# The second MLP product of three transformer layers from high and low fp32r parts, both made on VectorE

## What is computed

```python
h = gelu(xm @ W_mlp1 + b_mlp1)      # xm: normed and modulated x, [256, 256]; h: [256, 1024]
y = h @ W_mlp2 + b_mlp2             # the second product: the one that changes
x = x + gate * y
```

## Time and profile before

| | |
|---|---|
| median of 3 runs | 2873.33 us (2870.46 to 2873.42) |
| the profiled execution | 2874.42 us, of which the span from first to last instruction is 2872.6 us |
| PE busy | 2745.2 us, 96% of the span |
| PEld busy | 2279.8 us, 79% |
| DVE busy | 1732.0 us, 60% |
| ACT busy | 1548.3 us, 54% |
| POOL busy | 687.1 us, 24% |
| mean granted clock of TensorE | 0.974 of full speed |

### The profile page before, as it was taken

How to read it: one execution, slowest core, us unless ns; L and a number is a source line. 1 busy time by engine, 2 the same in 40 slices (tenths; PEclk the granted TensorE clock), 3 DMA queues, 4 the chain that set the end, 5 groups by cost and what they waited for, 6 DMA issues and landing times.

```text
span 2872.6 us, 61852 instructions
## 1 busy us (share of the span) xinstructions
PE 2745.2 (96%) x23508; PEld 2279.8 (79%) x23508; DVE 1732.0 (60%) x3584; ACT 1548.3 (54%) x2703; POOL 687.1 (24%) x759
## 2 busy tenths in 40 slices
PE   7999999995899999999999999999999999999998
PEld 6999999993577777777777777777777777777876
DVE  2444444434676776766766667667566666666642
ACT  3444444432456565665566656655566556556553
POOL 3433434321112212222222122222111111111111
PEclk8999999996899999999999999999999999999998
DMA  5122222104434444344464443554546535444421
GB/s 162 45 79 80 70 70 70 40 9 132 95 82 116 100 103 122 94 107 124 106 145 97 98 118 93 112 117 93 128 102 136 115 85 112 103 94 105 103 69 38
DMA packets 276950, 277.90 MB, mean 97 GB/s; under 512 B 90352, under 2 KB 206432, under 8 KB 276656
## 3 DMA queue, kind: packets, MB, share of 16 engines
q1 hardware_dynamic: 264752, 251.26, 36.8%
q10 hardware_dynamic: 11904, 22.68, 2.6%
HBM read 99.03 MB, written 29.56 MB: 45 GB/s over the span
## 4 chain that ended last, share of the span: by engine, by line
PE 64%; DVE 7%; issue 3%; ACT 2%; DMA 1%; SPq 0%; POOL 0%; POOLq 0%; DVEq 0%; ACTq 0%
PE gbank L3183 12%; PE obank L3028 10%; PE gbank L3028 7%; PE obank L3035 6%; PE score L3093 4%; PE obank L3113 4%; DVE m_a L2477 4%; PE obank L3159 3%; PE score L3079 3%; PE score L3142 2%; DVE x_a L2439 2%; PE gbank L3128 2%; PE obank L3128 2%; PE gbank L3019 2%; PE gbank L3043 2%
## 5 line engine op out<-in xcount | busy, mean ns | idle before, releaser
L1971 ACT ACTIVATE p_f<-score 128x1024 f32<-128x1024 f32 (+1 forms) x576 | 567.8, 1021 | 293.7 <-PE score L3093 264.6
L2477 DVE TENSOR_REDUCE m_a<-score 128x4 f32<-128x1024 f32 x384 | 459.9, 1219 | 159.0 <-PE score L3079 158.8
L3183 PE MATMUL gbank<-w,h_c 128*128 128x256 f32 x1536 | 387.9, 392 | 1.9 <-ACT h_c L1988 1.9
L3183 PEld LDWEIGHTS gbank<-w,h_c 128*128 128x128 f32 x1536 | 279.2, 191 | 44.9 <-ACT h_c L1988 2.3
L1150 PE MATMUL m_ps<-m_comb,m_w 128*128 128x256 f32 x2304 | 295.4, 284 | 1.5 <-PEq L254 1.5
L1150 PEld LDWEIGHTS m_ps<-m_comb,m_w 128*128 128x128 f32 x2304 | 279.9, 188 | 5.0 <-issue 3.6
L2487 DVE TENSOR_REDUCE m_b<-gbank 128x4 f32<-128x308 f32 x192 | 92.1, 480 | 265.1 <-PE gbank L3128 241.6
L823 ACT ACTIVATE m_hf<-m_ps,tab 128x256 f32<-128x256 f32 x192 | 80.7, 471 | 246.8 <-PE m_ps L1150 246.8
L1848 POOL TENSOR_TENSOR o_gated<-w_o,gate_a 128x512 f32<-128x512 f32 x48 | 62.3, 1298 | 591.0 <-PE obank L3035 591.0
L765 POOL TENSOR_TENSOR m_hhl<-m_hf,m_hhl 128x512 fp32r<-128x512 f32 x96 | 125.3, 1306 | 318.6 <-DVE m_hhl L989 318.6
L3113 PE MATMUL obank<-p_f,v_s 128*20 128x256 f32 x3072 | 199.9, 390 | 0.6 <-ACT p_f L1971 0.4
(11 more groups left out here) (287 smaller groups left out, 5446.0 us busy)
## 6 DMA issues: line engine op xcount, KB each, us to landing
q_cat<-q_hl SPq DMA_DIRECT2D x288, 128.0 KB, 3.7
k_cat<-k_hl SPq DMA_DIRECT2D x288, 128.0 KB, 4.0
qc_cat<-qc_hl SPq DMA_DIRECT2D x288, 128.0 KB, 3.1
split_L<-m_cut SPq DMA_DIRECT2D x24, 512.0 KB, 5.7
x_a<-x_after_L SPq DMA_DIRECT2D x48, 256.0 KB, 2.7
x_b<-x_after_L SPq DMA_DIRECT2D x48, 256.0 KB, 4.4
kc_cat<-kc_hl SPq DMA_DIRECT2D x288, 39.0 KB, 1.9
x_after_L<-y_c SPq DMA_DIRECT2D x32, 256.0 KB, 2.4
```

What stands on the lines that cost most here:

```text
L1971: e.activation(p_f[i % 4][0:n, :], score[i % 2].ap[0:n, :, :].rearrange("p h n -> p (h n)"), ACT.Exp, scale=SCALE).then_inc(ex.sem, 1)
L2477: e.tensor_reduce(m_a[:, :, i::NPAIR].rearrange("p t h -> p h t"), score[i % 2].ap[:, :, :].rearrange("p h (t k) -> p h t k", t=TT), AX.X, ...
L3183: mm = e.matmul(B_DOWN.ap[:, tt, :], h_c[:, k, tt * P:(tt + 1) * P], weights_of(d)["w2"][:, k, :], start=(k == 0), stop=(k == MC - 1))
```

## The change

ACT writes the gelu's result to a new small buffer `h_f` with two quarters; DVE casts each quarter to fp32r (`mlp_h_high`) and subtracts that from the exact value (`mlp_h_low`), both into a `h_c` with a high and a low plane. `down` makes three fp32r matmuls in place of each fp32 one, and waits per quarter. `up_act` waits until the low part two quarters earlier is made. The `w2` weights become four more pieces a layer: 36 pieces in place of 24, three per iteration of the mixture, still with two buffers; `w_down` is one buffer for all layers, loaded by ACT's queue at the start of `blocks` and at each change of layer.

```diff
+        def pieces_of(n):
+            return range(3 * n - 6, 3 * n - 3)
...
-                for i in range(2):
-                    store_piece(2 * n - 6 + i)
-                    load_piece(2 * n - 4 + i)
+                for k in pieces_of(n):
+                    store_piece(k - 2)
+                    load_piece(k)
...
-        h_c, y_c = sb("h_c", [P, MC, NT]), tile("y_c")
+        h_f, h_c, y_c = sb("h_f", [P, 2, 2, NT]), sb("h_c", [P, 2, MC, NT], F32R), tile("y_c")
...
             def up_act(u, i):
                 gelu = ACT.Gelu if layer(u) == 3 else ACT.Gelu_apprx_tanh
                 e.wait_ge(*S["C_hp"].at(u, i + 1))
-                if u and i == 0:
-                    e.wait_ge(*S["C_down"].at(u - 1))
+                if i >= 2:
+                    e.wait_ge(*S["C_hl"].at(u, i - 1))
+                elif u:
+                    e.wait_ge(*S["C_hl"].at(u - 1, i + 3))
...
+            def next_down(d):
+                if last_of_layer(d):
+                    e.wait_ge(*S["C_down"].at(d))
+                    load_split(layer(d) + 1, "down", "down", 8, (0, 1, 2, 3))
...
+            def mlp_h_high(c, i):
+                if not live(c):
+                    return
+                e.wait_ge(*S["C_h"].at(c, i + 1))
+                if c and i == 0:
+                    e.wait_ge(*S["C_down"].at(c - 1))
+                e.tensor_copy(h_c[:, 0, 2 * i:2 * i + 2, :], h_f[:, i % 2, :, :]).then_inc(S["C_hh"].sem, 1)
+
+            def mlp_h_low(c, i):
+                if live(c):
+                    e.wait_ge(*S["C_hh"].at(c, i + 1))
+                    e.tensor_tensor(h_c[:, 1, 2 * i:2 * i + 2, :], h_f[:, i % 2, :, :],
+                                    h_c[:, 0, 2 * i:2 * i + 2, :].bitcast(F32), ALU.subtract).then_inc(S["C_hl"].sem, 1)
...
             def down(d, j):
                 if not live(d):
                     return
+                tt, i = divmod(j, MC // 2)
                 if j == 0:
-                    e.wait_ge(*S["C_h"].at(d))
+                    weights_in(d, "down")
                     turn(B_DOWN, S["C_y"], d)
-                for i in (2 * j, 2 * j + 1):
-                    tt, k = divmod(i, MC)
-                    mm = e.matmul(B_DOWN.ap[:, tt, :], h_c[:, k, tt * P:(tt + 1) * P], weights_of(d)["w2"][:, k, :],
-                                  start=(k == 0), stop=(k == MC - 1))
+                if tt == 0:
+                    e.wait_ge(*S["C_hh"].at(d, i + 1))
+                for wp, xp in TERMS:
+                    if xp and tt == 0:
+                        e.wait_ge(*S["C_hl"].at(d, i + 1))
+                    for c in range(CC):
+                        mm = e.matmul(B_DOWN.ap[:, tt, :], h_c[:, xp, 2 * i + c, tt * P:(tt + 1) * P],
+                                      W["down"][:, i, wp, c, :], start=(i + wp + xp + c == 0),
+                                      stop=(i == MC // 2 - 1 and xp == 1 and c == CC - 1))
```

More of the change, by code:

```diff
@@ L806, in _ @@
                 hidden_low(g, 5)
-                for i in range(2):
-                    piece_low(2 * n - 4 + i)
+                for k in pieces_of(n):
+                    piece_low(k)
             gated_sum(NB - 1)
@@ L938, in _ @@
                 gate(g)
-                for i in range(2):
-                    piece_high(2 * n - 4 + i)
+                for k in pieces_of(n):
+                    piece_high(k)
         @block.vector
@@ L1904, in _ @@
             self_out_gated(4)
-            for n in range(6, 47):
-                q, a, c, d = n - 1, n - 3, n - 5, n - 6
+            context_rstd(4)
+            mlp_rstd(2)
+            for n in range(7, 47):
+                self_rstd(n - 1)
+                mlp_sum(n - 6)
+                self_residual(n - 3)
+                self_out_gated(n - 2)
+                mlp_residual(n - 5)
+                cross_rstd(n - 3)
+                cross_residual(n - 3)
                 if live(n) and n % NB == 0:
@@ L2145, in first_of_the_rest @@
                 load_split(1, "up1", "up", 4, (2, 3))
+                load_split(1, "down", "down", 8, (0, 1, 2, 3))
             e.wait_ge(s_w[1], 16 * n_w[1])
@@ L2267, in _ @@
             exp_table(1)
-            for n in range(6, 47):
-                q, m, a, b, c = n - 1, n - 2, n - 3, n - 4, n - 5
+            self_weights(4, 5)
+            self_heads(4, 0)
+            next_rest(6)
+            self_weights(4, 6)
+            self_weights(4, 7)
+            cross_max_high(3)
+            self_heads(4, 1)
+            mlp_modulated(2)
+            cross_weights(3, 0)
+            cross_weights(3, 1)
+            cross_weights(3, 2)
+            cross_heads(3, 0)
+            cross_weights(3, 3)
+            gelu_table(2)
+            context_out(4)
+            cross_heads(3, 1)
+            mlp_act(2, 0)
+            mlp_act(2, 1)
+            cross_keys_high(4)
+            mlp_act(2, 2)
+            for n in range(7, 47):
+                self_modulated(n - 1)
+                self_max_high(n - 2)
+                cross_x_out(n - 3)
+                mlp_act(n - 5, 3)
+                keys_high(n - 1)
+                cross_queries_high(n - 3)
+                exp_table(n - 5)
+                queries_high(n - 1)
+                self_weights(n - 2, 0)
+                self_weights(n - 2, 1)
+                self_weights(n - 2, 2)
+                self_weights(n - 2, 3)
+                self_weights(n - 2, 4)
                 if live(n) and n % NB == 0:
@@ L2825, in _ @@
             self_sum(3)
-            for n in range(6, 47):
-                p, q, m, a, b, c, d = n, n - 1, n - 2, n - 3, n - 4, n - 5, n - 6
+            cross_stats(3)
+            self_max(4, 7)
+            mlp_h_high(1, 2)
+            mlp_h_low(1, 2)
+            cross_normed(3)
+            self_x_high(5)
+            self_x_low(5)
+            self_max_low(4)
+            cross_x_low(3)
+            context_stats(4)
+            mlp_h_high(1, 3)
+            mlp_h_low(1, 3)
+            cross_heads_normed(2)
@@ new lines, in _ @@
+            keys_low(5)
+            cross_queries_low(3)
+            cross_sum(2)
+            queries_low(5)
+            mlp_stats(2)
+            cross_max(3, 0, 0)
+            cross_max(3, 0, 1)
+            context_normed(4)
+            cross_max(3, 1, 0)
+            cross_max(3, 1, 1)
+            mlp_normed(2)
+            cross_max(3, 2, 0)
+            cross_max(3, 2, 1)
+            cross_max(3, 3, 0)
+            cross_max(3, 3, 1)
+            for n in range(7, 47):
+                self_stats(n - 1)
+                cross_max_low(n - 4)
+                mlp_gated(n - 6)
+                self_normed(n - 1)
+                self_max(n - 2, 0)
+                self_max(n - 2, 1)
+                mlp_x_high(n - 5)
+                mlp_x_low(n - 5)
+                values_out(n - 2)
+                self_recips(n - 3)
+                self_max(n - 2, 2)
+                self_max(n - 2, 3)
+                self_max(n - 2, 4)
+                mlp_h_high(n - 5, 0)
+                mlp_h_low(n - 5, 0)
+                self_max(n - 2, 5)
+                mlp_h_high(n - 5, 1)
+                mlp_h_low(n - 5, 1)
+                self_heads_normed(n - 3)
+                self_max(n - 2, 6)
+                cross_recips(n - 4)
+                cross_keys_low(n - 3)
+                self_sum(n - 3)
+                cross_values_out(n - 3)
```

332 lines of the change are left out of this document (210 added, 122 removed).

## The result

The changed kernel takes **2910.76 us** (median; 2910.55 to 2913.43). The kernel before took 2871.89 us beside it (2866.67 to 2873.42). The ratio is **1.0135, 95% interval 1.0119 to 1.0152**: slower by 1.4%, about 39 us. Forecast were 2917 us, 2868 to 2952. The total is right, and the largest step of the blocks, the wait for `oT_a`, is right to 0.2 us. But that the sum came out is luck: a term of the mixture that was far too large stood against two costs that were not in it.

A forecast was written before the change was run, and what follows sets the result against it. PE was taken as the bound, with DVE only a few tenths of a microsecond ahead. Profiled 2874.42 us + 15.6 (blocks) + 23 (mixture) + 6 (`w_down` loads) - 1 (end) = 2918 us, 2917 for the median; range 2868 to 2952 us.

The forecast's parts named there:

- the wait for `oT_a`: In `blocks`, two pairs on DVE make PE wait 1.17 us in each full iteration, 49 us over 42.
- What `down` gives: In `down`, fp32r matmuls in place of fp32 save 1.20 us a unit, 57.6 us; 53.4 us kept.
- The wait for `xn_b`: In layers 1 and 2, the third pair makes PE wait another 0.6 us, 20 us over 28 iterations.
- Layer 3: In `blocks`, layer 3 has no `xn_b`, so only the first wait stands; iteration about 43.8 us, nothing lost.
- The third piece in the mixture: In the mixture, the third load holds ACT, so PE waits 1.9 us for `m_ctxT`; twelve iterations, 23 us (14 to 44).
- rival 3: In the mixture, the third piece lands in time, before PE needs `m_ctxT`: 2894 us; chance 0.13.
- The rest: Three `w_down` loads at 2 us each cost 6 us; the last unit's product at the end saves 1 us.
- Rival 1, the clock: Waits of 2 us in the mixture and 1.2 us in `blocks` bring half clock: 2941 or 2962 us; chance 0.12.
- Rival 2, DVE not late: DVE's pairs fall into gaps, no waits in `blocks`: 2848 us, or 2825 without the mixture's wait; chance 0.13.

The follow-up runs named there:

- spread: Changed kernel with the pairs of quarters 1, 2 and 3 moved later in DVE's order, same work; 2868.48 us, 0.9982 of the kernel before.
- swap: Changed kernel with PE's attention product of score pairs 4 and 5 moved ahead of the next unit's first two self-attention score products; 2900.70 us, 1.0108 of the kernel before.
- behind: Changed kernel with only quarter 1's pair moved on DVE, from ahead of `oT_a` to right behind it; 2999.53 us, 1.0431 of the kernel before.

## Why the prediction was right where it was, and wrong where it was not

- **What `down` gives.** Forecast: 1.20 us a unit, 0.1 us of it lost. The long group measured 3.18 us, not 3.00, the groups of six 0.96 as taken, so the groups save 1.02 us. The whole gain without the pairs is 1.25 us per iteration, nothing lost; where the other 0.2 us come from was not taken apart. In size right. (A tenth of 1.20 us over 42 iterations would be 5.0 us and not the 4.2 of the sum, and the other wait in the iteration is 0.59 us, not 0.44; neither changes anything.)
- **The wait for `oT_a`.** 1.17 us forecast, 1.00 measured; each instruction of DVE up to it came within 0.02 us of its forecast time. What differs is PE's due time: the products ahead end at 1678.26, not at 1678.10. (In the working, 1559.29 + 1.07 is 1560.36 and not 1560.39, which is less than a row can tell.) Right, and shown by `spread`.
- **The wait for `xn_b`.** 0.6 us forecast, 0.17 measured. DVE made up 0.2 us on the way (its third cast starts at 1684.29, not at 1684.50), and PE itself lost 0.24 us more before it. Together with `oT_a`, PE starts on `xn_b` 1.58 us late where 1.77 was forecast, so the iteration is 44.39 and not 44.6. In all, PE's list has 8.0 us of waits for `xn_b` where the term was 20; since PE itself lost time ahead of it, the blocks gained about 6 us of the 12 (28 iterations of 0.2 us).
- **Layer 3**: 43.8 forecast, 43.82 measured. Right.
- **The third piece in the mixture.** The step that failed is one choice: a landing of 5.0 us for the third load, from the middle of the earlier trace rows, although this load goes out nearly alone. It landed in 3.5 us, below every value of those rows. All else in that chain held: 1.9 us less the 1.5 is the 0.4 us that PE is late there. The sum also said that PE has no gap to give time back; an iteration of 34.94 us behind the last pieces, 37.00 before, gave back 2.1 us. The term was 23 us (14 to 44) and is 3 to 5. For the mixture, rival 3 is what happened; its total of 2894 us missed by the costs below.
- **The rest.** The w_down loads at the changes of layer cost 1 to 3 us each, as taken. Two costs had no term. The filling of `blocks` took 13 us more: the forecast counted the late pairs only from the steady part on (6 us of it), and the stretch with the first w_down load, set at 2 us, took 7, most of them PE's own work at a lower clock. And the rows of `k_cat` cost about 10 us (`swap` gave 8.6 us back, and 10 to 11 in the traces of iterations 4 to 43): that PE comes sooner was priced only against DVE's maxima, and not against the transfers, which showed no wait in any row of before because they came just in time.
- **Rival 1, the clock.** Behind the forty waits of 1.00 us it never fell. In iterations 4 to 43 it fell three times, for 3 to 10 us, each time behind a wait of 2.2 to 3.1 us for rows at a change of layer. The rule of the Trainium skill, "TensorE: Matmul & The Clock Gate", section "A second HAM failure mode: psum-queue depth-cycling", on a PE that idles briefly between groups was weighed there. This trace doesn't bear it out for single waits of 1 us; `behind`, with waits of 0.59, 1.04 and 1.32 us within 6 us, does, in 23 of its 40 iterations. In the filling the lower clock goes with 5 us more of busy time.
- **Rival 2, DVE not late.** Excluded by the brackets; `spread` shows that it was within reach of an order.

## What to carry to other kernels

Four pairs of instructions on an engine that is 60% busy cost 1.7 us an iteration while three of them stood ahead of the tiles that TensorE waits for, and 0.2 us with all but the first a few places further on, a third quarter of buffer and one product moved on PE (keys_first, 42.89 us, against 42.68 without any pair). So price an addition by who is waited for next behind it, and look for the place before judging the change. When the bounding engine becomes faster, list everything that it takes without a wait today, the transfers above all, since a margin that is just enough leaves no row. And before moving an instruction by a microsecond on VectorE, see what GpSimd runs at that moment, and look for an instruction that takes longer than others of its form.

## What the hardware showed that was not expected

- A 32-column cast and subtraction on DVE took 1.04 and 1.21 us in place of 0.18 and 0.19 while GpSimd ran 512-column operations, in 38 of the 48 units of `behind`, and in none of the other kernels; with GpSimd's operations cut to 16 columns they took 0.21 and 0.19. The second half of `x_a` took 1.35 to 1.38 us beside GpSimd's `y_c` in place of 0.4, in the kernels before and after alike. In the changed kernel DVE's operations with an input in PSUM ran beside the same GpSimd operations at their usual length (`x_b` 0.68 us).
- A single load of 256 KB beside one store landed in 3.2 to 4.1 us, twelve times; the loads of the kernel before, which go out as two loads and two stores in a row, took 4.3 to 6.8.
- Waits of 0.59 and 1.04 us with 0.63 us of work between them were followed by 3 to 7 us at half clock in 13 of 40 iterations and by full clock in others that look the same; waits of 1.00 and 0.59 us with 3.9 us of work between them never were.
